# Cross attention front: the normalisation moves from VectorE to ScalarE, six of eight query projections move into the steps, and the loads are reordered

## The reference

```python
def _L0_xattn_ref(q, k, v, Wq, bq, Wk, bk, Wv, bv, Wo, bo):
    qh = (q @ Wq + bq)...   # 16 heads of 16
    kh = (k @ Wk + bk)...
    vh = (v @ Wv + bv)...
    scores = einsum('bhqd,bhkd->bhqk', qh, kh) / sqrt(16)
    attn = softmax(scores)
    out = einsum('bhqk,bhkd->bhqd', attn, vh)
    return concat(out) @ Wo + bo

x = x + _L0_xattn_ref(_layernorm(x), ctx_512, ctx_512, ...)
x = x + _L0_attn_ref(_layernorm(x), ...)
x = x + _L0_ffn_ref(_layernorm(x), ...)
x = x + _L1_xattn_ref(_layernorm(x), ctx_512, ...)
...
```

## Time and profile before

| | |
|---|---|
| time before, median of 3 runs | 3862.19 us (3858.32 to 3870.57) |
| profiled execution, time | 3865.02 us |
| profiled execution, span | 3862.9 us |
| busy share of the span | PE 90%, PEld 75%, DVE 66%, ACT 56%, POOL 38% |
| first call of the cross attention | front from 0 to 63 us, steps to about 972 us |
| second call | front from 1706.8 to 1763 us, then its steps |

### The profile page before, as it was taken

One profiled execution on the slowest core, in us unless ns is written; L12 is line 12 of the kernel. 1 busy time (PEld: TensorE's weight loads), 2 busy tenths in 40 slices (PEclk: granted clock), 3 DMA queues, 4 the chain that ended last, 5 costly groups with the idle time before them and its releaser, 6 DMA issues. The chain is left out here.

```text
span 3862.9 us, 136176 instructions
## 1 busy us (share of the span) xinstructions
PE 3489.6 (90%) x58106; PEld 2887.8 (75%) x58107; DVE 2565.4 (66%) x4377; ACT 2167.3 (56%) x3419; POOL 1475.6 (38%) x1409
## 2 busy tenths in 40 slices
PE   8999999999785399939999999999769899999988
PEld 5888888888684266627888888888438788888867
DVE  5777777777543122246777777776769888888864
ACT  4666666666533022215666666666457788888732
POOL 4433333333031300053333333332028888888700
PEclk8999999999986699969999999999879999999989
DMA  2000010000005100020001000110001111111100
GB/s 79 29 29 29 29 37 29 29 29 21 11 1 225 68 31 31 30 85 28 29 29 38 29 29 29 33 34 3 26 19 47 41 43 44 42 42 42 39 24 22
DMA packets 60443, 148.34 MB, mean 38 GB/s; under 512 B 8242, under 2 KB 28754, under 8 KB 59506
## 3 DMA queue, kind: packets, MB, share of 16 engines
q1 hardware_dynamic: 56818, 131.70, 10.4%
q0 software_dynamic: 3072, 8.39, 0.7%
HBM read 123.29 MB, written 16.78 MB: 36 GB/s over the span
## 5 line engine op out<-in xcount | busy, mean ns | idle before, releaser
L743 ACT ACTIVATE x_probs<-x_score_ps 128x1024 f32<-128x1024 f32 (+1 forms) x896 | 814.8, 961 | 679.0 <-PE x_score_ps L592 670.8
L821 DVE TENSOR_REDUCE x_maxes<-x_misc_ps 128x1 f32<-128x512 f32 (+1 forms) x1792 | 1022.6, 628 | 27.5 <-PE x_misc_ps L503 21.8
L768 POOL CAST x_kT_hi<-x_kT 128x512 fp32r<-128x512 f32 (+1 forms) x448 | 254.7, 569 | 1227.7 <-ACT x_kT L671 1098.5
L2098 POOL TENSOR_TENSOR b_drive<-b_b_all,b_dtx 128x1024 f32<-128x1024 f32 x256 | 603.0, 2371 | 311.2 <-DVE b_dtx L2192 186.4
L2155 DVE TENSOR_TENSOR_SCAN b_state<-b_decay_ps,b_drive 128x512 f32<-128x512 f32 x512 | 603.0, 1213 | 44.9 <-issue 18.9
L586 PE MATMUL x_score_ps<-x_qz,x_kT 32*128 32x128 f32 x13312 | 591.3, 278 | 0.8 <-issue 0.7
L586 PEld LDWEIGHTS x_score_ps<-x_qz,x_kT 32*128 32x128 f32 x13312 | 502.1, 182 | 4.3 <-issue 2.4
L557 PE MATMUL x_misc_ps<-x_probs,x_v 128*32 128x64 f32 x26624 | 465.1, 221 | 0.0
L557 PEld LDWEIGHTS x_misc_ps<-x_probs,x_v 128*32 128x32 f32 x26624 | 392.8, 110 | 65.8 <-issue 23.2
L1929 PE MATMUL b_acc_ps<-ident,b_read 128*128 128x128 f32 x3072 | 413.8, 280 | 16.9 <-DVE b_xc L2178 16.9
L503 PE MATMUL x_misc_ps<-x_kT_hi,x_qz_hi 32*128 32x512 f32 (+1 forms) x2048 | 418.1, 403 | 4.6 <-ACT x_kT L671 3.4
(11 more groups left out here) (292 smaller groups left out, 5942.3 us busy)
## 6 DMA issues: line engine op xcount, KB each, us to landing
x_raw<-in_ctxT SPq DMA_DIRECT2D x64, 800.5 KB, 4.4
b_b_all<-b_b_rows SPq DMA_DIRECT2D x128, 256.0 KB, 3.3
m_w<-in_m_w SPq DMA_DIRECT2D x16, 704.0 KB, 19.0
m_w<-in_m_w SPq DMA_DIRECT2D x8, 768.0 KB, 19.7
m_slot_rows<-m_zero SPq DMA_DIRECT2D x1, 4992.0 KB, 17.1
m_block_rows<-m_slot_rows SPq DMA_DIRECT2D x39, 128.0 KB, 2.1
m_slot_out<-m_out SPq DMA_DIRECT2D x39, 128.0 KB, 1.7
x<-in_x SPq DMA_DIRECT2D x4, 512.0 KB, 6.7
```

The costliest lines, as they stand in the source:

```text
L743: nc.scalar.activation(probs[rows, s % 2, js, 0:n], score_ps[rows, js, 0:n], ACT.Exp).then_inc(exp_done, 1)
L821: nc.vector.tensor_reduce(maxes[:, c:c + m, j, k0 // NB], bank(op)[:, 0:m * even].rearrange("p (c k) -> p c k", c=m)[:, :, 0:kn], AX.X, AL ...
L2098: nc.gpsimd.tensor_tensor(drive[:, h % 3, :, :], b_all[:, k % 2:k % 2 + 1, :].broadcast_to([P, 2, NB]), dtx[:, half * 2:half * 2 + 2, :], ...
```

## The change

On DVE, `normalise` is replaced by `invert_root`: the reciprocal, and one scalar_tensor_tensor over 128 x 4 that makes `offset` = -mean * rstd. The normalised tiles are made by ACT, as an Identity activation with the column of `offset` as bias and that of `rstd` as scale. ACT's program begins with `root(0)`, the first four tiles, `root` of the other three groups, the load of the table for Exp, and then the copies of the first two pairs. The other twelve tiles, four at a time with the two copies behind them, stand after the maxima n = 0, 1 and 2.

PE's program begins with 16 transposes of ident. It then has two pairs, the first two queries, all four first shares of keys, and the maxima; after the maxima n = 0, 1 and 2 come two pairs each. The queries 2 to 7 go to the steps 1 to 6 as uses ("Q", n) of the ring, behind the values and ahead of `weigh`, and are read by ACT.

The loads go in another order: ident, x group 0, wk, context 0, wq, bq, mask, x group 1, wv, x groups 2 and 3, context 1. wk and wv have semaphores of their own, and POOL splits wv after the first four rounded keys instead of at the start.

```diff
-    QUERIES_AT = {0: (0, 1), 3: (2,), 4: (3,), 5: (4, 5), 6: (6, 7)}
+    WARM = 16
...
         if s + 2 < STEPS:
             ops.append(("V", s + 2))
+        if 0 < s < len(QUERIES) - 1:
+            ops.append(("Q", s + 1))
...
         def loads(sp):
-            load_x(sp, 0)
             if source is not None:
                 sp.dma_start(ident[:, :], source[1]).then_inc(ident_in, 16)
-            sp.dma_start(wk_sb[:, :], wk).then_inc(kv_in, 16)
-            sp.dma_start(wv_sb[:, :], wv).then_inc(kv_in, 16)
+            load_x(sp, 0)
+            sp.dma_start(wk_sb[:, :], wk).then_inc(k_in, 16)
+            sp.dma_start(raw[:, 0, :], ctxT[0, :, :]).then_inc(ctx_in[0], 16)
             sp.dma_start(wq_sb[:, :, :], wq).then_inc(q_in, 16)
             sp.dma_start(bq_sb[:, :], bq).then_inc(q_in, 16)
             sp.dma_start(mask[:, :], pair_mask).then_inc(q_in, 16)
             load_x(sp, 1)
-            sp.dma_start(raw[:, 0, :], ctxT[0, :, :]).then_inc(ctx_in[0], 16)
+            sp.dma_start(wv_sb[:, :], wv).then_inc(v_in, 16)
...
+            for n in range(WARM):
+                nc.tensor.transpose(score_ps[:, 2 + n % 2, 0:P], ident[:, :], ident[:, :])
             turn_rows(0)
             turn_rows(1)
-            for n in QUERIES_AT[0]:
-                project_queries(n)
-            project_keys(("K", 0, 0))
-            project_keys(("K", 0, 1))
-            turn_rows(2)
-            turn_rows(3)
-            project_keys(("K", 0, 2))
-            project_keys(("K", 0, 3))
+            pe.wait_ge(q_in, 48)
+            pe.wait_ge(copied, 2)
+            for n in range(KD):
+                first_queries(n)
+            for n in range(AHEAD):
+                project_keys(("K", 0, n))
             for n in range(NG):
                 for j in range(QUADS):
                     largest(("M", 0, n, j))
-                if n == 0:
-                    for pair in range(4, PAIRS):
-                        turn_rows(pair)
-                elif n <= NG - AHEAD:
+                if 0 < n <= NG - AHEAD:
                     project_keys(("K", 0, n + AHEAD - 1))
-                if n > 0:
-                    for q in QUERIES_AT.get(n, ()):
-                        project_queries(q)
+                if n < PAIRS // 2 - 1:
+                    turn_rows(2 * n + 2)
+                    turn_rows(2 * n + 3)
...
+                if 0 < s < len(QUERIES) - 1:
+                    project_queries(("Q", s + 1))
...
+            def normalise(t):
+                act.wait_ge(offset_done, t // UT + 1)
+                if t >= UT:
+                    act.wait_ge(transposed, (t - UT) // 2 + 1)
+                nc.scalar.activation(xn[:, t % UT, :], x_sb[:, t, :], ACT.Identity, bias=offset[:, t:t + 1],
+                                     scale=rstd[:, t:t + 1]).then_inc(xn_done, 1)
...
             root(0)
-            root(1)
+            for t in range(UT):
+                normalise(t)
+            for j in range(1, TURNS):
+                root(j)
+            act.wait_ge(std_done, TURNS)
+            nc.scalar.activation(warm[:, :], std[:, 0:1], ACT.Exp, scale=-1.0)
+            keep_rows(0)
+            keep_rows(1)
...
             for n in range(NG):
-                if n == 0:
-                    for pair in range(4, PAIRS):
-                        keep_rows(pair)
-                elif n <= NG - AHEAD:
+                if 0 < n <= NG - AHEAD:
                     keep_keys(("K", 0, n + AHEAD - 1))
-                if n > 0:
-                    for q in QUERIES_AT.get(n, ()):
-                        keep_queries(q)
+                if n < PAIRS // 2 - 1:
+                    for t in range(UT):
+                        normalise((n + 1) * UT + t)
+                    keep_rows(2 * n + 2)
+                    keep_rows(2 * n + 3)
...
-            def normalise(j):
+            def invert_root(j):
                 of = slice(j * UT, (j + 1) * UT)
                 dve.wait_ge(std_done, j + 1)
                 nc.vector.reciprocal(rstd[:, of], std[:, of]).then_inc(rstd_done, 1)
                 dve.wait_ge(rstd_done, j + 1)
-                for t in range(j * UT, (j + 1) * UT):
-                    if t >= UT:
-                        dve.wait_ge(transposed, (t - UT) // 2 + 1)
-                    nc.vector.tensor_scalar(xn[:, t % UT, :], x_sb[:, t, :], moments[:, t, 0:1], rstd[:, t:t + 1],
-                                            ALU.subtract, ALU.mult).then_inc(xn_done, 1)
+                nc.vector.scalar_tensor_tensor(offset[:, of], moments[:, of, 0], -1.0, rstd[:, of], ALU.mult, ALU.mult
+                                               ).then_inc(offset_done, 1)
```

More of the change, by code:

```diff
@@ L282, in cross_attention @@
     for op in ORDER:
-        reader = "act" if op[0] in "KV" else "dve"
+        reader = "act" if op[0] in "KVQ" else "dve"
         READS[reader] += 1
@@ L312, in cross_attention @@
         rstd = sb(f"{tag}_rstd", [P, NT])
+        offset = sb(f"{tag}_offset", [P, NT])
         eps = sb(f"{tag}_eps", [P, 1])
@@ L316, in cross_attention @@
         ident_in = sem(f"{tag}_ident_in")
-        kv_in = sem(f"{tag}_kv_in")
+        k_in = sem(f"{tag}_k_in")
+        v_in = sem(f"{tag}_v_in")
         q_in = sem(f"{tag}_q_in")
@@ L324, in cross_attention @@
         rstd_done = sem(f"{tag}_rstd_done")
+        offset_done = sem(f"{tag}_offset_done")
         xn_done = sem(f"{tag}_xn_done")
@@ L371, in split_context, with split_weights @@
             nc.gpsimd.tensor_tensor(raw_lo[of], raw[of], raw_hi[of].bitcast(F32), ALU.subtract).then_inc(raw_lo_done, 1)
[L373 to L378, removed]
+        def split_weights(pool, n):
+            full, high, low, arrived = ((wk_sb, wk_hi, wk_lo, k_in), (wv_sb, wv_hi, wv_lo, v_in))[n]
+            pool.wait_ge(arrived, 16)
+            nc.gpsimd.tensor_copy(high[:, :], full[:, :]).then_inc(w_hi_done, 1)
+            pool.wait_ge(w_hi_done, n + 1)
+            nc.gpsimd.tensor_tensor(low[:, :], full[:, :], high[:, :].bitcast(F32), ALU.subtract).then_inc(w_lo_done, 1)
         def split_of(b, key):
@@ L468, in turn_rows, with query, first_queries, project_queries @@
                 ins.then_inc(transposed, 1)
-            def project_queries(n):
+            def query(n, dst):
                 c, blk = QUERIES[n]
[L473 to L476, removed]
                 for k in range(KD):
-                    ins = nc.tensor.matmul(score_ps[:, 2 + n % 2, :], wq_sb[:, k, c * P:(c + 1) * P],
-                                           xnT[:, k, blk * NB:(blk + 1) * NB], start=k == 0, stop=k == KD - 1)
-                ins.then_inc(q_made, 1)
+                    ins = nc.tensor.matmul(dst, wq_sb[:, k, c * P:(c + 1) * P], xnT[:, k, blk * NB:(blk + 1) * NB],
+                                           start=k == 0, stop=k == KD - 1)
+                return ins
+            def first_queries(n):
+                query(n, score_ps[:, 2 + n % 2, :]).then_inc(q_made, 1)
+            def project_queries(op):
+                dst = open_bank(op)
+                query(op[1], dst).then_inc(misc_ready, 1)
             def project_keys(op):
@@ L693, in keep_rows, with keep_query, keep_queries @@
                                      ).then_inc(copied, 1)
-            def keep_queries(n):
-                c, blk = QUERIES[n]
-                act.wait_ge(q_made, n + 1)
-                nc.scalar.activation(qT[:, c, blk * NB:(blk + 1) * NB], score_ps[:, 2 + n % 2, :], ACT.Identity,
-                                     bias=bq_scaled[:, c:c + 1], scale=DH ** -0.5).then_inc(q_done, 1)
+            def normalise(t):
[4 more added lines that the diff above has]
+                                     scale=rstd[:, t:t + 1]).then_inc(xn_done, 1)
+            def keep_query(n, src):
+                c, blk = QUERIES[n]
+                return nc.scalar.activation(qT[:, c, blk * NB:(blk + 1) * NB], src, ACT.Identity,
+                                            bias=bq_scaled[:, c:c + 1], scale=DH ** -0.5)
+            def keep_queries(op):
+                made(act, op)
+                keep_query(op[1], bank(op)).then_inc(act_free, 1)
             act.wait_ge(eps_done, 1)
@@ L703, in _ @@
             root(0)
-            root(1)
+            for t in range(UT):
[6 more added lines that the diff above has]
+            keep_rows(1)
             act.wait_ge(q_in, 48)
             nc.scalar.activation(bq_scaled[:, :], bq_sb[:, :], ACT.Copy, scale=DH ** -0.5).then_inc(bq_done, 1)
-            keep_rows(0)
-            keep_rows(1)
-            root(2)
             act.wait_ge(bq_done, 1)
[L711 to L721, removed]
+            for n in range(KD):
+                act.wait_ge(q_made, n + 1)
+                keep_query(n, score_ps[:, 2 + n % 2, :]).then_inc(q_done, 1)
+            for n in range(AHEAD):
+                keep_keys(("K", 0, n))
             for n in range(NG):
-                if n == 0:
-                    for pair in range(4, PAIRS):
-                        keep_rows(pair)
```

(20 more changed lines are left out.)

4 lines of the change are left out of this document (2 added, 2 removed).

## The result

| | before | changed |
|---|---|---|
| median of 20 runs, us | 3860.45 (3854.37 to 3871.63) | 3877.06 (3868.00 to 3887.38) |
| ratio | | 1.0039, 95% interval 1.0030 to 1.0048 |
| span of the profiled execution, us | 3862.9 | 3875.2 |

The changed kernel is slower by 0.39%, about 15 us. The forecast was 16.8 us more.

What follows compares the result with a forecast made beforehand. Steps were taken as bound by PE (busy 906.5 of 909 us), fronts by no full engine. Fronts 6.0 + 3.4 - 2 x 6.8 = -4.2, queries +21.0, sum +16.8: 3862.2 to 3879.0 us, range 3860 to 3888.

Steps and rivals of the forecast that it cites:

- The price of the tile: ACT's tiles in the front: 0.60 us each, 0.49 from start to start, 2.07 us for four.
- The first query: Start of PE's first query in each call: 6.0 us later in the first, 3.4 us later in the second.
- the 2.0 us of the sum for the context ahead of it: First call's loads: 672 KB more ahead of x group 1 at 344 GB/s, landing at 11.1 instead of 9.12.
- From the query to the scores: Front of each call, first query to first scores: 41.7 us against 48.5, 6.8 us less.
- The loop as a chain of waits: Front, n = 1 and 2: maxima, keys, copy, tiles, transposes each wait for the one before; 6.73 us a turn, twice 13.5.
- The queries in the steps: Steps 1 to 6 of both calls: twelve queries paid in full on PE at 1.75 us, +21.0 us.
- The sum at step 7: Both calls' time to step 7's exponential, behind all queries, less the kernel before; set against the forecast's whole sum, +16.8 us.
- The fronts: Stretches up to the first scores in both calls: 6.0 + 3.4 - 2 x 6.8 = -4.2 us.
- The queries hidden in the steps: Rival 2: queries fill gaps in the steps and cost nothing, only -4.2 us is left, 3858.0 us; chance 0.11.
- The lower clock into step 0: Rival 3: values to scores takes 9.0 us, step 0 some 1.5 more, both calls; +7.8, 3886.8 us; chance 0.12.
- The clock at 1.00 through the maxima: Rival 1: front's loop falls from 6.73 to about 5.1 us, 6.3 us less a call, 3866.4 us; chance 0.17.
- The tiles on DVE: Front, by the skill's rule: four tiles at DVE's 1.4 us instead of 2.07, about 2 us a call less.

Runs made afterwards that it cites:

- the run with the old order of loads and late queries: Kernel before, with only the queries 2 to 7 moved to the steps 1 to 6; ratio 1.0016 to the kernel before.
- packed fronts: Changed kernel with pair copies first, tiles ahead, DVE's group 0 inversion earlier, context 0 behind x group 1; queries 2 to 7 in front 3844.5 us, in steps 3850.8.
- the run with the pair copies first: Changed kernel with ACT's first two pair copies ahead of the roots of groups 1 to 3 and the Exp table; ratio 1.0007 to the kernel before.
- the run with the tiles ahead: Changed kernel with ACT's tiles 8 to 15 made one group ahead, behind the pair copies of n = 0 and 1; ratio 1.0004 to the kernel before.
- no late queries: Changed kernel without the queries 2 to 7, later sequences reading the first block's queries; ratio 0.9977 to the kernel before.
- queries back in the front: Changed kernel with queries 2 to 7 moved from the steps into the front, after the maxima n = 1 to 4; 3862.1 against 3863.5 us, ratio 0.9999.

## Why the prediction was right

**The price of the tile** was right: 2.07 us for four, as worked out from three rows of copies.

**The first query** was forecast at 20.7 and 11.3 us and came at 19.8 and 11.5. In the first call x group 1 landed at 10.25, not 11.1. That is 1.1 us later than in the profile of the kernel before, but the run with the old order of loads and late queries had it at 10.20, so the 2.0 us of the sum for the context ahead of it are not shown; the packed fronts, with the context behind it, had it at 8.6 and 8.8. The 14.64 that the sum started from was an early execution: with nothing changed ahead of it, the first query came at 17.05 in that run. That this term came out near is in part luck. That the queries wait behind roots and table is shown by the run with the pair copies first. What the reordered loads cost was not tried alone.

**From the query to the scores**, term by term, first call: queries 5.8 (6.2 forecast), to the maxima n = 1 6.7 (6.5), two turns 13.8 (13.5), from n = 3 to the values 9.3 (8.9), values to scores 6.0 (6.6). The sum is 41.6, against 41.7. The loop as a chain of waits is shown by the run with the tiles ahead, which took 3.6 us out of each turn, the higher clock included. These terms came out close for the profiled execution; others of the same front were 2 to 3 us shorter, as said below. That the level would be 0.50 there is in the windows.

**The queries in the steps** were right in kind and nearly in size: 1.72 us each, 20.6 in all, against 1.75 and 21.0. The run that left them out and the one that put them back both show it.

**The sum at step 7** is 15.6, the ratio gives 15, the forecast was 16.8. The fronts gave 5.1 instead of 4.2, and the steps took 0.4 less. That the steps from step 7 on stay the same was taken without a word; in the profiled pair they took 3.3 us less over both calls.

**The rivals.** The queries hidden in the steps: out. The lower clock into step 0: it did not happen in the profiled execution, where PE was at 1.00 from about 59 us. The clock at 1.00 through the maxima did not happen to the changed kernel either. The price I gave it, 6.3 us a call, is not shown, but it has the right order: with the queries back in, the call that kept 1.00 was 4.1 us shorter than the one that lay at 0.50 for some 10 us.

**The tiles on DVE.** The prediction took the rule that the tiles would better stay on DVE to be worth about 2 us a call, and named DVE's lateness for the maxima as what speaks against it. Put back on DVE in the new order they gained nothing, with POOL's memset beside them and the maxima behind them; with the memset moved as well, the kernel was some 5 us below the change. So it is open whether the move to ACT helped or cost. What is shown to cost is the place of the queries, and the order in which roots, copies and tiles stand on ACT.

## What to carry to other kernels

Ask of work that is moved not whether its new place has slack on some engine, but which engine bounds that place: six matmul groups that filled waits in a front that was bound by latency cost 1.72 us each once they stood in a loop bound by PE. In a front, write the turn down as a chain (who waits for whom) before adding a link; making an input one turn ahead halved this one, with the help of a clock that then stayed up. And put what a later stage needs (roots, a table load) behind what the next engine is waiting for now.

## What the runs showed of the hardware that was not expected

The same front took different times in two calls of one execution, on identical instructions. The table has how long the granted clock was at 1.00 behind the first query (windows of 0.4 us):

| kernel | query to scores, calls 1 and 2, us | clock falls to 0.50, us behind the first query |
|---|---|---|
| changed | 41.6, 41.5 | 12.4, 12.4 |
| no late queries | 41.8, 38.9 | 12.8, 16.8 |
| no transposes of ident | 39.6, 39.0 | 18.4, 17.2 |
| queries back in the front | 43.9, 39.8 | 12.4 (back up at 19.2), not at all |

A part of the spread of some 0.2% either way between runs may be this; that is inferred, not tried.

At the start of a trace the clock that the profile gives is to be doubted: in the first call of the changed kernel it reads 1.00 from the start, but the eight query records took 6.34 us, as in the second call (6.27), where it reads 0.50 for the first 5.6 us of them, and not 3.70 as at 1.00.

TensorE's granted clock can rise on transposes alone. In the second call of the packed front sixteen of them, and the eight of the rows behind them, took it from 0.50 to 1.00 before the queries; the eight of the rows by themselves did not. In the second call of the changed kernel they had done so too, but PE then waited 4.9 us for ACT's copies and was back at 0.50 when the queries came. The effect was worth 2.9 us once the queries followed at once, in one pair of executions, and nothing that could be measured before.

The Trainium skill (SBUF — State Buffer, Who interferes with whom) says that a tensor_scalar on DVE can take the ports that it shares with GpSimd, and that the one then blocks the other for a whole instruction. The trace agrees: four tiles took 5.45 us beside the memset and 2.67 without it. It also says that ScalarE never waits; ACT's four tiles took 2.07 and 2.06 us, with POOL's splits and casts beside them. The memset never stood beside ACT's tiles here, but a copy by ACT that started inside it, at 32.41, took 0.60 us as elsewhere.
